# The last stage of a two-branch attention kernel: two layer-norm loops and an output loop merged into one loop over row tiles

## The chip, the cores and the metric

The kernel runs on one Trainium2 chip, the same program on eight cores, each with one batch element of 2048 rows by 1024 columns. The metric is the device time in microseconds (us) of the slowest core. The engines are TensorE (PE), VectorE (DVE), ScalarE (ACT), GpSimd (POOL) and SyncE (SP); here SP issues nearly all transfers. The profile is one execution on the slowest of the cores (core 5).

## The reference, cut to what matters

```python
xn = _layernorm(x, axis=-1)
s = _L0_attn_ref(xn, ...)          # 16 causal heads, then Wo, then a layer norm (eps 1e-5)
g = _silu(_L0_ffn_ref(xn, ...))    # six attention nodes of 8 heads, then a layer norm (eps 1e-6)
x = x + s * g
```

The last stage of the kernel computes, for each row, the layer norm of `y` (what the causal attention and its output product leave), the layer norm of `n5` (what the sixth node leaves), Silu of the second, their product, and the sum with the row of x.

## The kernel before, in words

Six nodes (projections, attention, output product) run first, then the causal attention ("L0"), then the product with Wo. Everything is kept feature-major, 128 features on the partitions and 2048 rows along them. Node 5 is stored to the DRAM tensor `n5_sp` and `y` to `y_sp`, both bf16 and feature-major. The trace calls `n5_sp` by the name `n_sp`.

The last stage starts when `y` is stored and has four parts, one behind the other.

1. `build_gam` (L1020 to L1038) spreads the norm's two parameter rows over the 128 partitions: for each row a 4 KB load into `lrow` (which is `fio[2]`), two matmuls with a row of ones into `ps[3]`, and two DVE copies into `gamT`. Each load waits for the copies of the row before it.
2. `ln_apply_loop` (L1040 to L1096) runs over the 16 row tiles of `y`. For each, SP issues a transposing load of 128 rows into `attb[0]` or `attb[1]` (L1043), DVE takes the sum (L1048) and the sum of squares (L1051, whose full result goes to PSUM as scratch), makes mean and variance in five operations on one column, ACT takes Ln and Exp of that column (L1073, L1076) for the reciprocal root, and DVE finishes with one small product (L1079) and three passes over the tile (L1082, L1086, L1090), the last into `slot[Dv]`. The load of tile tc waits for the last pass of tile tc-2.
3. `build_gam` and `ln_apply_loop` again, for `n5`, into the same `gamT` and into `slot[B]`; the first parameter load waits for all tiles of part 2.
4. All 16 Silu on ACT (L1105), and the output loop: load of 128 rows of x into `fio[0]` or `fio[1]` (L1112), product of the two norms into `fio[2]` (L1115), sum with x in place (L1118), store of `fio[2]` (L1122). The product of the next tile waits until the store has landed, because there is one `fio[2]`. The load of x for tile tc waits for the sum of tile tc-2, but it is issued on SP behind the store of tile tc-1, which waits for the sum of tile tc-1.

`P.op` (L46) appends an instruction to the list of its engine together with the waits it needs, and `finalize` (L72, the line that the waits carry in the trace is L73) writes each list out as it stands: a wait is an instruction of its own ahead of the operation. So every engine, SP and its transfers among them, works strictly in the order in which the Python code calls `P.op`. `trq` and `pln`, the names under which transfers are issued, are both `"sync"`.

`wstage` is a pair of fp32 staging tiles of 128 by 1024 for weights; by the last stage no weight is left to load.

Of the kernel before, what the change touches and what calls it, by code (L numbers as in the profile page):

```python
# [8 lines left out]
BF16 = mybir.dt.bfloat16  # L9
AF = mybir.ActivationFunctionType  # L10
ALU = mybir.AluOpType
AX = mybir.AxisListType

D = 1024
KC = 8
# [79 lines left out]
def build_nc(T=2048, debug=False):  # L95
    TC = T // 128
# [27 lines left out]
    n5_sp = nc.dram_tensor("n5_sp", [D, T], BF16, kind="Internal")  # L124
    y_sp = nc.dram_tensor("y_sp", [D, T], BF16, kind="Internal")
    dbg = {}
    if debug:
        for c in (0, 1):
# [11 lines left out]
    P = Prog()  # L140
# [5 lines left out]
    wstage = [e(nc.sbuf_tensor(f"wstage{i}", [128, 1024], F32)) for i in range(2)]  # L146
    qbuf = e(nc.sbuf_tensor("qbuf", [128, T], BF16))
    kbuf = e(nc.sbuf_tensor("kbuf", [128, T], BF16))
    attb = [e(nc.sbuf_tensor(f"attb{i}", [128, max(PW, 1024)], BF16))
            for i in range(4)]  # L150
# [17 lines left out]
    stat = e(nc.sbuf_tensor("stat", [128, 16], F32))  # L168
    gamT = e(nc.sbuf_tensor("gamT", [128, 2 * 1024], BF16))
# [4 lines left out]
    ps = [e(nc.psum_tensor(f"ps{i}", [128, 1024], F32)) for i in range(4)]  # L174
    ps_last = {0: None, 1: None, 2: None, 3: None}
# [4 lines left out]
    def slot_written(i, ch, tok):  # L180
        slot_w[i][ch] = tok if isinstance(tok, list) else [tok]
        slot_r[i] = []
# [11 lines left out]
    def tchunk(s, tc, d0=0, dw=1024):  # L194
        return slot[s][:, tc * 1024 + d0: tc * 1024 + d0 + dw]

    dge, pln, trq = "gpsimd", "sync", "sync"

    def pser():
# [4 lines left out]
        out=ewrow[0:1, 0:18],  # L204
        in_=W["few"].ap().rearrange("a b -> (a b)")[None, :]),
        waits=pser(), inc="P", inc_n=16)
    t_aw = P.op(trq, lambda g: g.dma_start(
        out=ewrow[0:1, 18:24], in_=W["fact"].ap()[None, :]),
        waits=pser(), inc="P", inc_n=16)
# [6 lines left out]
        waits=[t_io1], inc="tDVE")  # L216
    t_t128 = P.op("vector", lambda v: v.tensor_scalar(
        t128[:, :], fio[0][:, 0:128], 0.0, None, ALU.is_ge),
        waits=[t_io1], inc="tDVE")
# [6 lines left out]
        out=vec_stage[:, 0:128],  # L226
        in_=W["fbe"].ap().rearrange("a (c p) -> (a c) p", p=128)[0:128, :]),
        waits=pser(), inc="P", inc_n=16)
# [49 lines left out]
    for i in range(TC):  # L278
        b = i % 2
# [738 lines left out]
                               spill_sem="SPy")  # L1018
    wbuf_free[wo_b].append(t_y)

    def build_gam(i0, i1, ready):
        toks = []
        for j, i in enumerate((i0, i1)):
            tr = P.op(trq, lambda g, i=i: g.dma_start(
                out=lrow[0:1, 0:1024], in_=W[vps[4 + i]].ap()[None, :]),
                waits=pser() + list(ready) + toks, inc="P", inc_n=16)
            for h2 in range(2):
                tm = P.op("tensor", lambda t, j=j, h2=h2: t.matmul(
                    ps[3][:, h2 * 512:(h2 + 1) * 512], ones_f32r[0:1, :],
                    lrow[0:1, h2 * 512:(h2 + 1) * 512], start=True, stop=True),  # L1030
                    waits=[tr, ps_last[3], t_on2], inc="tPE")
                te = P.op("vector", lambda v, j=j, h2=h2: v.tensor_copy(
                    gamT[:, j * 1024 + h2 * 512: j * 1024 + (h2 + 1) * 512],
                    ps[3][:, h2 * 512:(h2 + 1) * 512]), waits=[tm], inc="tDVE")
                ps_last[3] = te
                toks.append(te)
        return toks

    def ln_apply_loop(dst_slot, src_sp, src_ready, eps, gam_toks):
        toks = []  # L1040
        for tc in range(TC):
            b = tc % 2
            tk = P.op(trq, lambda g, tc=tc, b=b, a=src_sp: g.dma_start(  # L1043
                out=attb[b][:, 0:1024], in_=a.ap()[:, tc * 128:(tc + 1) * 128],
                transpose=True),
                waits=list(src_ready) + attb_free[b], inc=f"T{b}", inc_n=16)
            q0 = 8 + b * 4
            t1 = P.op("vector", lambda v, b=b, q0=q0: v.reduce_sum(  # L1048
                stat[:, q0:q0 + 1], attb[b][:, 0:1024], axis=AX.X),
                waits=[tk] + list(gam_toks), inc="tDVE")  # L1050
            t4 = P.op("vector", lambda v, b=b, q0=q0: v.scalar_tensor_tensor(  # L1051
                ps[b][:, 0:1024], attb[b][:, 0:1024], 1.0,
                attb[b][:, 0:1024], ALU.mult, ALU.mult,
                accum_out=stat[:, q0 + 1:q0 + 2]),
                waits=[tk, ps_last[b]], inc="tDVE")
            ps_last[b] = t4
            tm = P.op("vector", lambda v, q0=q0: v.tensor_scalar(
                stat[:, q0:q0 + 1], stat[:, q0:q0 + 1], 1.0 / D, None,
                ALU.mult), waits=[t1], inc="tDVE")
            tq = P.op("vector", lambda v, q0=q0: v.tensor_tensor(  # L1060
                stat[:, q0 + 2:q0 + 3], stat[:, q0:q0 + 1],
                stat[:, q0:q0 + 1], ALU.mult), waits=[tm], inc="tDVE")
            tv = P.op("vector", lambda v, q0=q0: v.tensor_scalar(
                stat[:, q0 + 1:q0 + 2], stat[:, q0 + 1:q0 + 2], 1.0 / D,
                None, ALU.mult), waits=[t4], inc="tDVE")
            tv = P.op("vector", lambda v, q0=q0: v.tensor_tensor(
                stat[:, q0 + 1:q0 + 2], stat[:, q0 + 1:q0 + 2],
                stat[:, q0 + 2:q0 + 3], ALU.subtract),
                waits=[tv, tq], inc="tDVE")
            tv = P.op("vector", lambda v, q0=q0, eps=eps: v.tensor_scalar(  # L1070
                stat[:, q0 + 1:q0 + 2], stat[:, q0 + 1:q0 + 2], 1.0, eps,
                ALU.mult, ALU.add), waits=[tv], inc="tDVE")
            t6 = P.op("scalar", lambda s, q0=q0: s.activation(  # L1073
                stat[:, q0 + 2:q0 + 3], stat[:, q0 + 1:q0 + 2], AF.Ln),
                waits=[tv], inc="tACT")
            t7 = P.op("scalar", lambda s, q0=q0: s.activation(  # L1076
                stat[:, q0 + 1:q0 + 2], stat[:, q0 + 2:q0 + 3], AF.Exp,
                scale=-0.5), waits=[t6], inc="tACT")
            t7 = P.op("vector", lambda v, q0=q0: v.tensor_tensor(  # L1079
                stat[:, q0 + 3:q0 + 4], stat[:, q0:q0 + 1],  # L1080
                stat[:, q0 + 1:q0 + 2], ALU.mult), waits=[t7], inc="tDVE")
            t8 = P.op("vector", lambda v, b=b, q0=q0: v.tensor_scalar(  # L1082
                attb[b][:, 0:1024], attb[b][:, 0:1024],
                stat[:, q0 + 1:q0 + 2], stat[:, q0 + 3:q0 + 4],
                ALU.mult, ALU.subtract), waits=[t7], inc="tDVE")
            t9 = P.op("vector", lambda v, b=b: v.tensor_tensor(  # L1086
                attb[b][:, 0:1024], attb[b][:, 0:1024], gamT[:, 0:1024],
                ALU.mult), waits=[t8], inc="tDVE")
            t10 = P.op("vector", lambda v, b=b, ds=dst_slot, tc=tc:
                       v.tensor_tensor(  # L1090
                tchunk(ds, tc), attb[b][:, 0:1024], gamT[:, 1024:2048],
                ALU.add), waits=[t9], inc="tDVE")
            attb_free[b] = [t10]
            slot_written(dst_slot, tc % max(KC, TC), t10)
            toks.append(t10)
        return toks  # L1096

    fio_free[2] = ps_last[2]
    gam_s = build_gam(0, 1, y_spills)
    s_toks = ln_apply_loop(Dv, y_sp, y_spills, 1e-5, gam_s)  # L1100
    gam_g = build_gam(2, 3, s_toks)
    g_toks = ln_apply_loop(B, n5_sp, n5_spills, 1e-6, gam_g)
    gs_toks = []
    for tc in range(TC):
        gs_toks.append(P.op("scalar", lambda s, tc=tc: s.activation(  # L1105
            tchunk(B, tc), tchunk(B, tc), AF.Silu), waits=[g_toks[tc]],
            inc="tACT"))

    out_toks = []
    for tc in range(TC):  # L1110
        b = tc % 2
        tx = P.op(pln, lambda g, tc=tc, b=b: g.dma_start(  # L1112
            out=fio[b][:, :], in_=x_in.ap()[tc * 128:(tc + 1) * 128, :]),
            waits=[fio_free[b]], inc=f"X{b}", inc_n=16)
        t1 = P.op("vector", lambda v, tc=tc: v.tensor_tensor(  # L1115
            fio[2][:, :], tchunk(Dv, tc), tchunk(B, tc), ALU.mult),
            waits=[s_toks[tc], gs_toks[tc], fio_free[2]], inc="tDVE")
        t2 = P.op("vector", lambda v, b=b: v.tensor_tensor(  # L1118
            fio[2][:, :], fio[2][:, :], fio[b][:, :], ALU.add),
            waits=[tx, t1], inc="tDVE")  # L1120
        fio_free[b] = t2
        td = P.op(pln, lambda g, tc=tc: g.dma_start(  # L1122
            out=out_t.ap()[tc * 128:(tc + 1) * 128, :], in_=fio[2][:, :]),
            waits=[t2], inc="OUT", inc_n=16)
        fio_free[2] = td
        out_toks.append(td)
# [41 lines left out]
```

How the kernel before makes its waits and increments, by code:

```python
                def emit(eng):  # L70
                    for it in items:
                        if it[0] == "w":
                            eng.wait_ge(sems[it[1]], it[2])
                        else:
                            ins = it[1](eng)
                            if it[2] is not None:
                                ins.then_inc(sems[it[2]], it[3])
```

## Time and profile before

| | |
|---|---|
| runs of the kernel before | 7833.9 and 8154.16 us, median 7994.03 |
| the profiled execution | 7833.9 us |
| its span on the slowest core (5) | 7831.2 us |
| spans of the eight cores | 7773.6 to 7831.2 us |
| mean granted TensorE clock of the cores | 0.842 to 0.846 |
| the last stage on core 5, first parameter load to end of the span | 7500.8 to 7831.2, 330.4 us |
| busy over the span | PE 75%, PEld 24%, DVE 28%, ACT 35%, POOL 5% |

A row of the timeline gives the start in us, the duration in us, the engine, the line of the kernel, the operation, what it writes and reads, and in brackets how long the engine stood idle before it and what ended that. SPq is SP issuing a transfer: its duration is that of the issuing, not of the transfer.

### The profile page before, as it was taken

To read this page: it belongs to the slowest core of one execution; us is meant where nothing else is said; L and a number is where in the kernel's file an instruction comes from. 1 tells how busy PE (TensorE), PEld (TensorE's weight loads), DVE (VectorE), ACT (ScalarE), POOL (GpSimd) and SP (SyncE) were. 2 spreads that over 40 slices of the span, in tenths; PEclk is the share of its full clock that TensorE was granted. 3 is DMA by queue.
4 is the path that set the end of the run, shared out by engine and by line. 5 is a ranking of instruction groups with operands and counts; after the bars stand their busy time and mean duration, and the time that the engine had idled before them with its cause. 6 is when DMAs were issued, how large, how long until landed. Compare 5 with 4: busy or idle time off the path is not lost.

```text
span 7831.2 us, 62343 instructions; the slowest of 8 cores (7773.6 to 7831.2 us)
## 1 busy us (share of the span) xinstructions
PE 5850.8 (75%) x21827; PEld 1918.4 (24%) x21827; DVE 2198.8 (28%) x3068; ACT 2735.9 (35%) x2612; POOL 364.7 (5%) x354
## 2 busy tenths in 40 slices
PE   0677787777987779877789777897777878778830
PEld 0222233222332223322234222342222311111110
DVE  3133321333213332133321333213332122222155
ACT  0155432544225443155431454214552123333301
POOL 0100011000010000100011000110001100000000
PEclk9989998888998989988999888998888955555665
DMA  2300032000420004200033000230003100000013
GB/s 74 104 1 0 3 105 65 0 1 27 113 76 1 1 14 114 88 0 1 1 85 109 0 1 1 81 112 1 1 1 90 56 0 0 0 0 0 0 46 105
DMA packets 204568, 289.37 MB, mean 37 GB/s; under 512 B 141576, under 2 KB 141800, under 8 KB 204268
## 3 DMA queue, kind: packets, MB, share of 16 engines
q1 hardware_dynamic: 204236, 285.39, 12.4%
q8 instruction: 186, 3.05, 0.2%
q14 instruction: 114, 0.93, 0.0%
q0 software_dynamic: 32, 0.00, 0.0%
HBM read 218.24 MB, written 33.55 MB: 32 GB/s over the span
## 4 chain that ended last, share of the span: by engine, by line
PE 67%; DVE 18%; issue 6%; ACT 4%; DMA 4%; SPq 1%; DVEq 1%; POOL 0%; ACTq 0%; POOLq 0%
PE ps L384 17%; PE ps L564 9%; PE ps L869 8%; DVE attb L615 6%; PE ps L625 6%; PE ps L634 5%; PE ps L447 5%; PE ps L610 5%; DVE stat L515 4%; PE ps L595 3%; PE ps L586 3%; PE ps L508 3%; DVE attb L499 2%; DMA fio<-x 2%; ACT attb L675 1%
## 5 line engine op out<-in xcount | busy, mean ns | idle before, releaser
L675 ACT ACTIVATE attb<-ps,negM,scal 128x1024 bf16<-128x1024 f32 x1536 | 1766.8, 1199 | 1931.8 <-DVE negM L531 1435.6
L384 PE MATMUL ps<-slot,wbuf 128*128 128x512 bf16 x6144 | 1367.7, 383 | 223.3 <-POOL wbuf L358 199.2
L564 PE MATMUL ps<-qbuf,kbuf 128*128 128x512 bf16 x3072 | 1023.6, 424 | 173.0 <-ACT attb L675 150.2
L615 DVE TENSOR_TENSOR attb<-attb 128x1024 bf16<-128x1024 bf16 x768 | 534.8, 696 | 1787.6 <-PE ps L610 1771.7
L384 PEld LDWEIGHTS ps<-slot,wbuf 128*128 128x128 bf16 x6144 | 604.5, 99 | 971.8 <-issue 263.3
L869 PE MATMUL ps<-slot,wbuf 128*128 128x512 bf16 x3072 | 693.1, 385 | 82.8 <-POOL wbuf L358 82.8
L625 PE MATMUL ps<-attb,ones_bf 128*1 128x512 bf16 x1536 | 477.0, 393 | 360.6 <-DVE attb L615 354.9
L508 PE MATMUL ps<-attb,ones_sq 128*128 128x512 bf16 (+1 forms) x512 | 238.5, 564 | 609.6 <-DVE attb L499 608.4
L358 POOL CAST wbuf<-wstage 128x1024 bf16<-128x1024 f32 x344 | 363.1, 1059 | 5760.6 <-DVE kbuf L880 3655.9
L675 ACT ACTIVATE attb<-ps,negM 128x1024 bf16<-128x1024 f32 (+7 forms) x384 | 328.2, 863 | 664.0 <-PE ps L564 662.2
L610 PE MATMUL ps<-attb,slot 128*128 128x512 bf16 x1536 | 497.1, 408 | 21.3 <-DVE slot L737 21.3
L634 PE MATMUL ps<-attb,slot 128*128 128x512 bf16 x1536 | 481.5, 396 | 0.0
L564 PEld LDWEIGHTS ps<-qbuf,kbuf 128*128 128x128 bf16 x3072 | 278.6, 104 | 789.9 <-issue 632.4
L447 PE MATMUL ps<-wbuf,slot 128*128 128x512 bf16 x1792 | 394.3, 382 | 42.6 <-POOL wbuf L358 41.5
L515 DVE TENSOR_REDUCE stat<-ps 128x1 f32<-128x1024 f32 x256 | 313.6, 1225 | 391.2 <-PE ps L508 391.2
L869 PEld LDWEIGHTS ps<-slot,wbuf 128*128 128x128 bf16 x3072 | 299.8, 99 | 465.5 <-issue 122.2
L407 ACT ACTIVATE slot<-ps,beT 128x1024 bf16<-128x1024 f32 x120 | 133.7, 1114 | 700.6 <-PE ps L384 700.6
L564 PE MATMUL ps<-slot 64*128 64x512 bf16 x768 | 361.6, 579 | 16.7 <-ACT attb L675 16.5
L415 DVE TENSOR_SCALAR slot<-ps,beT 128x1024 bf16<-128x1024 f32 x120 | 154.1, 1284 | 721.6 <-PE ps L384 721.6
L880 DVE CAST qbuf<-ps 128x1024 bf16<-128x1024 f32 x96 | 117.6, 1225 | 678.6 <-PE ps L869 678.6
L595 PE MATMUL ps<-attb,slot 128*64 128x512 bf16 (+3 forms) x656 | 294.1, 530 | 0.0
L586 PE MATMUL ps<-attb,ones_bf 128*1 128x512 bf16 (+3 forms) x656 | 283.2, 514 | 2.3 <-DVE attb L686 2.3
(101 smaller groups left out, 2531.4 us busy)
## 6 DMA issues: line engine op xcount, KB each, us to landing
wstage<-fWe SPq DMA_DIRECT2D x120, 512.0 KB, 4.3
wstage<-fWv SPq DMA_DIRECT2D x48, 512.0 KB, 4.2
wstage<-fWq SPq DMA_DIRECT2D x48, 512.0 KB, 4.2
wstage<-fWk SPq DMA_DIRECT2D x48, 512.0 KB, 4.1
wstage<-fWo SPq DMA_DIRECT2D x48, 512.0 KB, 4.2
slot<-n_sp SPq DMA_DIRECT2D x40, 512.0 KB, 9.0
fio<-x SPq DMA_DIRECT2D x32, 512.0 KB, 4.1
n_sp<-slot SPq DMA_DIRECT2D x32, 512.0 KB, 2.6
```

The lines of the kernel that those rows point to most:

```text
L384: t.matmul(ps[pb][:, sg * SEG:(sg + 1) * SEG], wtile(ws, kc, do * 128, 128), fchunk(ss, kc, th * TW + sg * SEG, SEG), start=(kc == 0), sto ...
L447: pb=pb, ws=wslot, ss=src_slot: t.matmul(ps[pb][:, half * 512:(half + 1) * 512], fchunk(ss, kc, tc * 128, 128), wtile(ws, kc, half * 512, ...
L515: t_mx = P.op("vector", lambda v, dst=dst: v.reduce_max(stat[:, dst:dst + 1], ps[3][:, 0:NH], axis=AX.X), waits=[t_nm], inc="tDVE")
L564: t_s = P.op("tensor", lambda t, kc=kc, sg=sg, pb=pb: t.matmul(ps[pb][:, sg * PSEG:(sg + 1) * PSEG], kf_tile_fn(kc), q_rhs_fn(sg * PSEG, P ...
L586: l_first=l_first, l_last=l_last: t.matmul(ps[3][0:1, o:o + w], ones_bf[:, 0:1], attb[ab][:, o:o + w], start=l_first, stop=l_last),
L595: av_stop=av_stop: t.matmul(ps[2][obase:obase + dh, o:o + w], v_tile_fn(kc), attb[ab][:, o:o + w], start=av_first, stop=av_stop, tile_posi ...
L610: first=(j0 == 0): t.matmul(ps[2][obase:obase + dh, o:o + w], v_tile_fn(kc0), attb[a0][:, o:o + w], start=first, stop=False, tile_position ...
L615: t_pr = P.op("vector", lambda v, a0=a0, a1=a1: v.tensor_tensor(attb[a0][:, 0:PW], attb[a0][:, 0:PW], attb[a1][:, 0:PW], ALU.add), waits=[ ...
L625: t.matmul(ps[3][0:1, o:o + w], ones_bf[:, 0:1], attb[a0][:, o:o + w], start=first, stop=last),
L634: last=(j1 == n_kc - 1): t.matmul(ps[2][obase:obase + dh, o:o + w], v_tile_fn(kc1), attb[a1][:, o:o + w], start=False, stop=last, tile_pos ...
L675: off=off: s.activation(attb[ab][:, off:PW], ps[pb][:, off:PW], AF.Exp, bias=negM[:, nc_:nc_ + 1], scale=scale_col),
L869: src_sl=src_sl: t.matmul(ps[pb][:, sg * SEG:(sg + 1) * SEG], wtile(wsl, kc, h * 128, 128), fchunk(src_sl, kc, th * TW2 + sg * SEG, SEG), ...
```

## The change

The three loops of the last stage become one. For each row tile the new loop norms the tile of `y` (`ln_tile` with `attb[0]`/`attb[1]`, `ps[0]`/`ps[1]`, statistics in columns 0 to 7), norms the tile of `n5` (with `attb[2]`/`attb[3]`, `ps[2]`/`ps[3]`, columns 8 to 15), takes Silu of it, loads x, multiplies, adds and stores. Both parameter pairs are spread ahead of the loop; the second pair goes into `gamT2`, which is `wstage[0]` read as bf16. The operations on a tile are the same as before, in the same order within a tile; the order over the tiles, and with it each engine's list and SP's list of transfers, is new. The wait for the parameters moves from the sum (L1048) to the transposing load.

```diff
+    gamT2 = wstage[0].ap().bitcast(BF16)
-    def ln_apply_loop(dst_slot, src_sp, src_ready, eps, gam_toks):
-        toks = []
-        for tc in range(TC):
-            b = tc % 2
-            tk = P.op(trq, lambda g, tc=tc, b=b, a=src_sp: g.dma_start(
-                out=attb[b][:, 0:1024], in_=a.ap()[:, tc * 128:(tc + 1) * 128],
-                transpose=True),
-                waits=list(src_ready) + attb_free[b], inc=f"T{b}", inc_n=16)
...
+    def ln_tile(dst_slot, src_sp, src_ready, eps, g0, g1, tc, ab, psb, q0,
+                gtoks):
+        b = tc % 2
+        tk = P.op(trq, lambda g, tc=tc, ab=ab, a=src_sp: g.dma_start(
+            out=attb[ab][:, 0:1024], in_=a.ap()[:, tc * 128:(tc + 1) * 128],
+            transpose=True),
+            waits=list(src_ready) + attb_free[ab] + list(gtoks),
+            inc=f"T{ab}", inc_n=16)
...
-    gam_s = build_gam(0, 1, y_spills)
-    s_toks = ln_apply_loop(Dv, y_sp, y_spills, 1e-5, gam_s)
-    gam_g = build_gam(2, 3, s_toks)
-    g_toks = ln_apply_loop(B, n5_sp, n5_spills, 1e-6, gam_g)
-    gs_toks = []
-    for tc in range(TC):
-        gs_toks.append(P.op("scalar", lambda s, tc=tc: s.activation(
-            tchunk(B, tc), tchunk(B, tc), AF.Silu), waits=[g_toks[tc]],
-            inc="tACT"))
+    gam_s = build_gam(0, 1, y_spills, lambda j, h2: gamT[
+        :, j * 1024 + h2 * 512: j * 1024 + (h2 + 1) * 512])
+    gam_g = build_gam(2, 3, list(n5_spills) + gam_s, lambda j, h2: gamT2[
+        :, j * 1024 + h2 * 512: j * 1024 + (h2 + 1) * 512],
+        wgate=[wstage_free[0]])
+    fio_free[2] = gam_g[-1]
 
     out_toks = []
     for tc in range(TC):
         b = tc % 2
+        s_tok = ln_tile(Dv, y_sp, y_spills, 1e-5, gamT[:, 0:1024],
+                        gamT[:, 1024:2048], tc, b, b, b * 4, gam_s)
+        g_tok = ln_tile(B, n5_sp, n5_spills, 1e-6, gamT2[:, 0:1024],
+                        gamT2[:, 1024:2048], tc, 2 + b, 2 + b, 8 + b * 4,
+                        gam_g)
+        gs_tok = P.op("scalar", lambda s, tc=tc: s.activation(
+            tchunk(B, tc), tchunk(B, tc), AF.Silu), waits=[g_tok],
+            inc="tACT")
         tx = P.op(pln, lambda g, tc=tc, b=b: g.dma_start(
             out=fio[b][:, :], in_=x_in.ap()[tc * 128:(tc + 1) * 128, :]),
             waits=[fio_free[b]], inc=f"X{b}", inc_n=16)
         t1 = P.op("vector", lambda v, tc=tc: v.tensor_tensor(
             fio[2][:, :], tchunk(Dv, tc), tchunk(B, tc), ALU.mult),
-            waits=[s_toks[tc], gs_toks[tc], fio_free[2]], inc="tDVE")
+            waits=[s_tok, gs_tok, fio_free[2]], inc="tDVE")
```

The sum and the store that follow are as before.

## Rows read from the trace of the kernel before

**Rows 1.** The page: span, and the chain that ended last, by engine.
```profile
span 7831.2 us, 62343 instructions; the slowest of 8 cores (7773.6 to 7831.2 us)
...
PE 67%; DVE 18%; issue 6%; ACT 4%; DMA 4%; SPq 1%; DVEq 1%; POOL 0%; ACTq 0%; POOLq 0%
```

**Rows 2.** Busy time by stretch: PE, PEld, DVE, ACT, POOL; clock, DMA share, GB/s.
```profile
7516.10:7617.20 101.10, 0.00 (x0) 0.00 (x0) 79.53 (x192) 6.49 (x32) 0.00 (x0) 0.50 0.18 37
...
7632.60:7734.60 102.00, 0.00 (x0) 0.00 (x0) 79.43 (x192) 8.87 (x35) 0.00 (x0) 0.50 0.19 41
7734.60:7831.20 96.60, 0.00 (x0) 0.00 (x0) 39.28 (x33) 14.15 (x15) 0.00 (x0) 0.50 0.50 168
```

**Rows 3.** Timeline of the first norm loop: tiles 0 and 1 of `y`.
```profile
7516.12 1.22 DVE L1048 TENSOR_REDUCE stat<-attb 128x1 f32<-128x1024 bf16 x1
...
7519.26 0.15 DVE L1070 TENSOR_SCALAR stat<-stat 128x1 f32<-128x1 f32 x1
7519.51 0.20 ACT L1073 ACTIVATE stat<-stat 128x1 f32<-128x1 f32 x1 [28.60 <-DVE stat L1070]
...
7521.90 0.69 DVE L1090 TENSOR_TENSOR slot<-attb,gamT 128x1024 bf16<-128x1024 bf16 x1
7522.50 1.21 DVE L1048 TENSOR_REDUCE stat<-attb 128x1 f32<-128x1024 bf16 x1
```

**Rows 4.** Timeline of the output loop: tiles 0 and 1, and the last sum.
```profile
7734.66 1.23 DVE L1115 TENSOR_TENSOR fio<-slot 128x1024 f32<-128x1024 bf16 x1
7735.99 1.23 DVE L1118 TENSOR_TENSOR fio<-fio 128x1024 f32<-128x1024 f32 x1
7737.29 0.37 SPq L1122 DMA_DIRECT2D out<-fio  x1
7737.71 0.42 SPq L1112 DMA_DIRECT2D fio<-x  x1
...
7742.52 1.23 DVE L1118 TENSOR_TENSOR fio<-fio 128x1024 f32<-128x1024 f32 x1 [1.03 <-DMA fio<-x]
...
7826.92 1.23 DVE L1118 TENSOR_TENSOR fio<-fio 128x1024 f32<-128x1024 f32 x1 [0.38 <-DMA fio<-x]
```

**Rows 5.** Waits of the last stage: who waited for what, us, times, longest.
```profile
DVE fio L1115 <- DMA out<-fio: 42.6, 14, 3.1
DVE stat L1079 <- ACT stat L1076: 22.6, 32, 1.0
DVE fio L1118 <- DMA fio<-x: 8.5, 15, 1.0
```

**Rows 6.** Timeline around the second parameter spread.
```profile
7617.27 0.25 SPq L1024 DMA_DIRECT2D fio<-fln_g  x1
...
7632.65 1.22 DVE L1048 TENSOR_REDUCE stat<-attb 128x1 f32<-128x1024 bf16 x1
```

**Rows 7.** The transposing load's own view: issue ns min/median/max, time to landing.
```profile
L1043 SPq DMA_TRANSPOSE attb<-y_sp x16: 1145/1146/1207, 7508.8 to 7604.6; - x16
...
DMA to landing us min/median/max: 2.9/3.2/4.4
```

**Rows 8.** The page's transfers: the node reloads, KB each, us to landing.
```profile
slot<-n_sp SPq DMA_DIRECT2D x40, 512.0 KB, 9.0
```

**Rows 9.** Timeline around the only two table loads of the kernel.
```profile
36.60 0.15 DVE L308 TENSOR_SCALAR stat<-stat 128x1 f32<-128x1 f32 x1
36.84 1.28 ACT L311 ACT_TABLE_LOAD   x1 [36.84 <-DVE stat L308]
...
38.73 0.16 DVE L317 TENSOR_TENSOR stat<-stat 128x1 f32<-128x1 f32 x1 [1.98 <-ACT stat L314]
...
7731.99 0.20 ACT L1076 ACTIVATE stat<-stat 128x1 f32<-128x1 f32 x1
7732.21 1.28 ACT L1105 ACT_TABLE_LOAD   x1
...
7733.51 15.25 ACT L1105 ACTIVATE slot<-slot 128x1024 bf16<-128x1024 bf16 x16
```

More of the change, by code:

```diff
@@ L1019, in build_nc, with build_gam @@
     wbuf_free[wo_b].append(t_y)
-    def build_gam(i0, i1, ready):
+    gamT2 = wstage[0].ap().bitcast(BF16)
+    def build_gam(i0, i1, ready, dst_fn, wgate=()):
         toks = []
@@ L1027, in build_gam @@
             for h2 in range(2):
-                tm = P.op("tensor", lambda t, j=j, h2=h2: t.matmul(
+                tm = P.op("tensor", lambda t, h2=h2: t.matmul(
                     ps[3][:, h2 * 512:(h2 + 1) * 512], ones_f32r[0:1, :],
@@ L1032, in build_gam @@
                 te = P.op("vector", lambda v, j=j, h2=h2: v.tensor_copy(
-                    gamT[:, j * 1024 + h2 * 512: j * 1024 + (h2 + 1) * 512],
-                    ps[3][:, h2 * 512:(h2 + 1) * 512]), waits=[tm], inc="tDVE")
+                    dst_fn(j, h2), ps[3][:, h2 * 512:(h2 + 1) * 512]),
+                    waits=[tm] + list(wgate), inc="tDVE")
                 ps_last[3] = te
@@ L1037, in build_gam @@
         return toks
-    def ln_apply_loop(dst_slot, src_sp, src_ready, eps, gam_toks):
-        toks = []
-        for tc in range(TC):
-            b = tc % 2
-            tk = P.op(trq, lambda g, tc=tc, b=b, a=src_sp: g.dma_start(
-                out=attb[b][:, 0:1024], in_=a.ap()[:, tc * 128:(tc + 1) * 128],
-                transpose=True),
-                waits=list(src_ready) + attb_free[b], inc=f"T{b}", inc_n=16)
[L1047 to L1096, printed above, removed]
@@ L1098, in build_nc @@
-    fio_free[2] = ps_last[2]
-    gam_s = build_gam(0, 1, y_spills)
-    s_toks = ln_apply_loop(Dv, y_sp, y_spills, 1e-5, gam_s)
-    gam_g = build_gam(2, 3, s_toks)
-    g_toks = ln_apply_loop(B, n5_sp, n5_spills, 1e-6, gam_g)
-    gs_toks = []
-    for tc in range(TC):
-        gs_toks.append(P.op("scalar", lambda s, tc=tc: s.activation(
-            tchunk(B, tc), tchunk(B, tc), AF.Silu), waits=[g_toks[tc]],
-            inc="tACT"))
+    def ln_tile(dst_slot, src_sp, src_ready, eps, g0, g1, tc, ab, psb, q0,
[6 more added lines that the diff above has]
+            inc=f"T{ab}", inc_n=16)
+        t1 = P.op("vector", lambda v, ab=ab, q0=q0: v.reduce_sum(
+            stat[:, q0:q0 + 1], attb[ab][:, 0:1024], axis=AX.X),
+            waits=[tk], inc="tDVE")
+        t4 = P.op("vector", lambda v, ab=ab, q0=q0, psb=psb:
+                  v.scalar_tensor_tensor(
+            ps[psb][:, 0:1024], attb[ab][:, 0:1024], 1.0,
+            attb[ab][:, 0:1024], ALU.mult, ALU.mult,
+            accum_out=stat[:, q0 + 1:q0 + 2]),
+            waits=[tk, ps_last[psb]], inc="tDVE")
+        ps_last[psb] = t4
+        tm = P.op("vector", lambda v, q0=q0: v.tensor_scalar(
+            stat[:, q0:q0 + 1], stat[:, q0:q0 + 1], 1.0 / D, None,
+            ALU.mult), waits=[t1], inc="tDVE")
+        tq = P.op("vector", lambda v, q0=q0: v.tensor_tensor(
+            stat[:, q0 + 2:q0 + 3], stat[:, q0:q0 + 1],
+            stat[:, q0:q0 + 1], ALU.mult), waits=[tm], inc="tDVE")
+        tv = P.op("vector", lambda v, q0=q0: v.tensor_scalar(
+            stat[:, q0 + 1:q0 + 2], stat[:, q0 + 1:q0 + 2], 1.0 / D,
+            None, ALU.mult), waits=[t4], inc="tDVE")
+        tv = P.op("vector", lambda v, q0=q0: v.tensor_tensor(
+            stat[:, q0 + 1:q0 + 2], stat[:, q0 + 1:q0 + 2],
+            stat[:, q0 + 2:q0 + 3], ALU.subtract),
+            waits=[tv, tq], inc="tDVE")
+        tv = P.op("vector", lambda v, q0=q0, eps=eps: v.tensor_scalar(
+            stat[:, q0 + 1:q0 + 2], stat[:, q0 + 1:q0 + 2], 1.0, eps,
+            ALU.mult, ALU.add), waits=[tv], inc="tDVE")
+        t6 = P.op("scalar", lambda s, q0=q0: s.activation(
+            stat[:, q0 + 2:q0 + 3], stat[:, q0 + 1:q0 + 2], AF.Ln),
+            waits=[tv], inc="tACT")
+        t7 = P.op("scalar", lambda s, q0=q0: s.activation(
+            stat[:, q0 + 1:q0 + 2], stat[:, q0 + 2:q0 + 3], AF.Exp,
+            scale=-0.5), waits=[t6], inc="tACT")
+        t7 = P.op("vector", lambda v, q0=q0: v.tensor_tensor(
+            stat[:, q0 + 3:q0 + 4], stat[:, q0:q0 + 1],
+            stat[:, q0 + 1:q0 + 2], ALU.mult), waits=[t7], inc="tDVE")
+        t8 = P.op("vector", lambda v, ab=ab, q0=q0: v.tensor_scalar(
+            attb[ab][:, 0:1024], attb[ab][:, 0:1024],
+            stat[:, q0 + 1:q0 + 2], stat[:, q0 + 3:q0 + 4],
+            ALU.mult, ALU.subtract), waits=[t7], inc="tDVE")
+        t9 = P.op("vector", lambda v, ab=ab, g0=g0: v.tensor_tensor(
+            attb[ab][:, 0:1024], attb[ab][:, 0:1024], g0,
+            ALU.mult), waits=[t8], inc="tDVE")
+        t10 = P.op("vector", lambda v, ab=ab, g1=g1, ds=dst_slot, tc=tc:
+                   v.tensor_tensor(
+            tchunk(ds, tc), attb[ab][:, 0:1024], g1,
+            ALU.add), waits=[t9], inc="tDVE")
+        attb_free[ab] = [t10]
+        slot_written(dst_slot, tc % max(KC, TC), t10)
+        return t10
```

## The prediction

> **What bounds the kernel now.** I read the page first. Over the whole span the chain that ended last is mostly PE, with DVE second [rows 1]; but the change touches nothing ahead of the last stage, so the share that counts is that stage's own, 330.4 of 7831.2 us. The windows cut by its parts come next: 101.1 us for the norm of `y`, 102.0 for the norm of `n5`, 96.6 for the output loop [rows 2], and two parameter spreads of 15.4 us each (7617.27 to 7632.65, [rows 6]; the first runs from 7500.8 to 7516.1 in the same way). PE does nothing in the three loops. Then the timeline, loop by loop.
>
> In the norm loops DVE is busy 79.5 of 101.1 us [rows 2], one tile takes 101.1/16 = 6.32 us, and the one wait of any size is for Ln and Exp (22.6 us over 32 tiles, 0.71 each, [rows 5]). The loads cost nothing: two pairs of buffers let them run a tile ahead. So these loops are bound by DVE's own list.
>
> The output loop is different. DVE is busy 39.3 of 96.6 us there. From the first sum at 7735.99 to the last at 7826.92 there are 15 pitches of 6.06 us [rows 4], of which the product and the sum take 2.5; 42.6 us go to waiting for the store of the one `fio[2]` and 8.5 to waiting for x [rows 5]. SP issues the store, then the next load of x, which lands after the store does: issue at 7737.71, sum at 7742.52. This loop is bound by one turn of DMA per tile. That is what a merged loop can hide, and the sum has to show what it exposes in exchange.
>
> **Cost per part.** *Parameters.* The second spread is not removed, it moves ahead of the loop. It still waits for the first one's copies, nothing runs beside it, and it still takes 15.4 us. The first load of `y` is queued behind its second row's load on SP and lands while the copies still run. The first sum then starts at 7516.12 + 15.4 = 7531.5. Against before: nothing gained, nothing lost.
>
> *Norm of a tile.* Same instructions. From the start of the first sum to the end of the last pass is 7516.12 to 7521.90 + 0.69, that is 6.47 us [rows 3]; where another tile follows, 6.32.
>
> *Product, sum, x and store.* 1.33 to the sum's start, 1.23 for the sum, 2.56 together [rows 4]. The store has a whole tile of DVE work to land in, and x is loaded at the head of the tile: both waits of [rows 5] go. That removes (42.6 + 8.5) us plus the tile-0 wait for Silu.
>
> *The transposing load.* Here the cover goes. SP's list is now: load `y`(tc), load `n5`(tc), x(tc), store(tc), load `y`(tc+1). The store waits for the sum of tile tc, the last thing DVE does in a tile, and everything behind it on SP waits too, although `attb` is free long before. DVE's next instruction is the sum over `y`(tc+1), so DVE and ACT stand still for a whole turn. Its length: 0.07 from the end of the sum to the store (7737.22 to 7737.29), 0.42 until the next transfer can be issued (7737.71) [rows 4], the landing, and 0.1 to DVE. A landing took 2.9 to 4.4 us, median 3.2 [rows 7], but mostly with the queue idle; here a 512 KB store is just ahead and a second transpose just behind. Below, 2.9 us; above, the 4.4 plus 1.5, since the output loop moves two such transfers per 6.06 us at a DMA share of 0.50, so one keeps the engines for 0.25 x 6.06 = 1.5 us [rows 2, 4]. I take 3.8, nearer the median, because issuing a transpose alone takes 1.15 us [rows 7], in which most of the store drains. Together 4.4 us per tile, 15 times (tile 0 is covered by the parameters). The load of `n5` is issued 1.15 us later and needed 7 us later: hidden.
>
> *Table loads.* Before, ACT did all Ln and Exp, then one table load, then 16 Silu. The kernel has two table loads, of 1.28 us, Ln and Exp sharing one table [rows 9]. Now Silu of tile tc stands between Exp of tile tc and Ln of tile tc+1: one load before each Silu, 16, and one before each Ln but the first, 15. Are they hidden while ACT idles? The first load says no: ACT stood idle for 36.84 us, with nothing to do, and began the load only when DVE's column came, because the load sits behind the wait; DVE then waited 1.98 us for the result in place of the usual 0.7 [rows 5, 9]. So each of the 31 is on the path at 1.28 us. Below, nothing, if they ran ahead of the wait. Above, I take a second load's time per switch, 1.28 more. I choose 1.28, as both loads in the trace are followed at once by their ACTIVATE (7732.21 + 1.28, next at 7733.51).
>
> On this the Trainium skill speaks against the change. "ScalarE: Activation LUTs", section "Rules for kernel authors", says to group functions by table set, and "What ACT_TABLE_LOAD costs" gives 1283 ns for the load plus about 1380 ns of drain, 2.66 us per switch. The trace agrees on the 1.28 and shows no drain: the load at 7732.21 starts 0.02 us after Exp ends. By the page's figure the estimate would be 31 x 1.38 = 43 us more than mine.
>
> *Silu.* Before, 15 of 16 ran under the output loop's stalls (15.25 us for 16, [rows 9]). Now the product waits for its own: 0.1 from DVE to ACT (as L1070 to L1073, [rows 3]), 1.30 for load and start, about 1.0 for one ACTIVATE (15.25/16 = 0.95 in a row, a little more for one alone), 0.1 back: 2.5 us.
>
> **The sum.** A tile takes 4.39 (SP, store, load) + 6.32 + 1.28 (norm of `y` with a table load) + 6.47 (norm of `n5`) + 2.50 (Silu) + 2.56 = 23.52 us. Before, the same work took (7828.15 - 7516.12 - 15.5)/16 = 18.5 us per tile over the three loops. Tile 0 has neither the load wait nor the first table load: 17.85. The last sum ends at 7531.5 + 17.85 + 15 x 23.52 = 7902.2; before it ended at 7828.15. That is 74 us more. Hiding the transfers of the output loop gives back 6.06 - 2.56 = 3.5 us per tile; the exposed transposing load costs 4.4, the two table loads 2.6, the uncovered Silu 1.2, and the last 0.3 are ends that no longer overlap.
>
> The profiled execution took 7833.9 us, so I expect 7833.9 + 74 = 7908 us, 0.94% more. The shown median, 7994.03, lies halfway between two runs that are 320 us apart; the profiled one is the lower. Ahead of the last stage nothing changes, so the same shift holds for either: 8068 on the median.
>
> **Rivals.**
>
> *A. As summed*, small loss, 7908; with the transpose at 2.9 or at 5.9 and everything else the same, 15 x 0.9 = 14 less, 7894, or 15 x 2.1 = 32 more, 7940.
>
> *B. Table loads hidden.* If they ran ahead of the wait during ACT's idle time, 31 x 1.28 = 40 us less: 7868. For it: ACT is idle in most of each tile. Against: the load at 36.84 [rows 9].
>
> *C. Each switch costs twice the load.* 40 us more: 7948. For it: the trace has no case of a load between Silu and Ln, and only two loads. Against: no gap beside either. The skill's rule above is this case, with its 1.38.
>
> *D. Not slower: the transposes run ahead.* If SP issued the load of tile tc+1 before the store of tile tc, the 4.4 us go: the tile is 19.13, the end at 7531.5 + 17.85 + 15 x 19.13 = 7836.3, 8 us later than before, 7842, which no one can tell from before. It decides at a per-tile pitch of 18.5. Against it: SP's list as `finalize` writes it, and the same order in the output loop, where x waits behind the store each time [rows 4]. If the change were to win, this is where, and even then the table loads eat it.
>
> *E. Slower by over 2%.* That needs 157 us, 83 beyond my sum, 5.5 per tile: the transpose would have to land in 9.3 us. Transfers in this kernel do land as late as 9.0 us in the median, where many 512 KB loads are queued [rows 8]. With 9.0 it is 7833.9 + 74 + 15 x 5.2 = 7986. Against it: there is but one store ahead here, and the DMA share falls from 0.50 to less than half of that.
>
> **How the numbers follow.** A 0.66, B 0.10, C 0.12, D 0.04, E 0.04; 0.04 for what I have not seen. The likeliest is A, 7908, and its own range is 7890 to 7945. For 8 in 10 the range takes in B and C, 7860 below and 7965 above. The shown times of before are a median over runs so far apart that the time after may be one too; the like shift of that median gives 8068, so I set the upper end at 8085. About 2% is what a measurement of this kernel can tell from no change: A to D lie within it, E lies at its edge, and the spread of the runs adds a little. Faster 0.02, within 0.90, slower 0.08.
>
> **What would show each step.** In the profile after: 32 table loads in all, each beginning when DVE's column or tile arrives; DVE waiting about 2 us for Exp in the norm of `y` and 0.7 in that of `n5`; the product waiting about 2.5 us for Silu and never for the store; the sum never waiting for x; SP issuing store, transpose, transpose, x in one bunch per tile, and the first DVE sum of a tile about 4.4 us behind the last sum; a pitch of about 23.6 us; the stage from the first parameter load to the end about 405 us in place of 330. I would be wrong if the pitch came out at or under 18.5, if the table loads started while ACT idled, or if the landing of a transpose were doubled by the store.

## The result and the profile after

The changed kernel is slower by 1%: the ratio of its time to that of the kernel before is 1.0098, with a 95% interval of 1.0078 to 1.0118. Five of its executions took 7904 to 7910 us, and the profiled one of before 7833.9 us. The medians over all executions, 8026.66 us (14) against 8154.16 (12), point the other way only because they hold executions in which the cores of one die ran at a lower granted clock (the profiled one of the changed kernel is such a one, 0.824 to 0.831 on cores 0 to 3); the ratio leaves those out.

The profile after is read on core 5: span 7904.3 us, clock 0.841. To compare last stages, one measure serves for all kernels: from the issue of the last store of `y` to the end of the span. It is 333.9 us before (mean of the eight cores, 329.9 to 335.9) and 410.3 after (407.9 to 412.2). TensorE does little in this stage, and its length does not follow the clock: 409.0 to 412.2 us on cores 0 to 3, 407.9 to 411.3 on cores 4 to 7 (0.836 to 0.841). The last stage holds 76.4 us of difference; 0.98% of 7834 is 77. So the stage accounts for the whole loss as closely as it is known, and nothing ahead of the stage was changed.

Busy time by stretch on core 5 of the changed kernel: the parameter spreads, then the merged loop (columns as in [rows 2]).

```profile
7496.88:7527.22 30.34, 16.33 (x16) 3.98 (x16) 5.45 (x8) 0.00 (x0) 0.00 (x0) 0.50 0.05 10
7527.22:7904.30 377.08, 0.00 (x0) 0.00 (x0) 199.51 (x417) 69.65 (x111) 0.00 (x0) 0.50 0.24 66
```

DVE works about as long as before (199.5 us against 79.5 + 79.4 + 39.3 in [rows 2]), in 377 us instead of 300. ACT is busy for 69.7 us, where it was busy for 29.5. The DMA share is 0.24 in the mean, where the output loop alone had 0.50.

The waits of the changed kernel, on core 5, from the last store of `y` to the end:

```profile
ACT L1075 <- DVE stat L1072: 159.5, 15, 11.0
ACT stat L1075 <- DVE stat L1072: 139.1, 17, 45.1
DVE stat L1049 <- DMA attb<-y_sp: 68.1, 15, 4.9
DVE fio L1121 <- ACT slot L1115: 41.5, 16, 2.6
DVE stat L1081 <- ACT stat L1078: 41.4, 32, 2.0
```

Against [rows 5]: the waits for the store and for x are gone, all 51 us. In their place DVE waits 68.1 us for the transposes of `y`, 41.5 us for Silu, and 41.4 instead of 22.6 for Exp. One turn from tile to tile, in the timeline of core 5:

```profile
7657.59 0.69 DVE L1092 TENSOR_TENSOR slot<-attb,wstage 128x1024 bf16<-128x1024 bf16 x1
7658.36 1.28 ACT L1115 ACT_TABLE_LOAD   x1 [2.59 <-DVE slot L1092]
7659.66 1.06 ACT L1115 ACTIVATE slot<-slot 128x1024 bf16<-128x1024 bf16 x1
7660.89 1.23 DVE L1121 TENSOR_TENSOR fio<-slot 128x1024 f32<-128x1024 bf16 x1 [2.60 <-ACT slot L1115]
7662.22 1.23 DVE L1124 TENSOR_TENSOR fio<-fio 128x1024 f32<-128x1024 f32 x1
7663.51 0.34 SPq L1128 DMA_DIRECT2D out<-fio  x1
7663.90 1.50 SPq L1044 DMA_TRANSPOSE attb<-y_sp  x1
7665.44 1.27 SPq L1044 DMA_TRANSPOSE attb<-n_sp  x1
7666.75 0.56 SPq L1118 DMA_DIRECT2D fio<-x  x1
7668.37 1.22 DVE L1049 TENSOR_REDUCE stat<-attb 128x1 f32<-128x1024 bf16 x1 [4.93 <-DMA attb<-y_sp]
...
7671.75 1.28 ACT L1075 ACT_TABLE_LOAD   x1 [11.03 <-DVE stat L1072]
...
7673.64 0.16 DVE L1081 TENSOR_TENSOR stat<-stat 128x1 f32<-128x1 f32 x1 [1.97 <-ACT stat L1078]
```

Read it for who stands still. After the last pass over the tile, DVE has nothing until Silu is done, and Silu starts with a table load. After the sum at 7662.22 DVE has nothing again: SP wakes, issues the store, and only then the transpose that DVE needs next. The bracket of the second table load is the telling one: ACT had been idle for 11.03 us and still began the load only when DVE's column arrived. Each of these gaps is in series with the next, because each engine has one list and the tile's last operation stands ahead of the next tile's first in all of them.

### The profile page after: what moved, and what is told of

It is laid out like the page before. It is cut to its first block, busy times and chain, and to the rows that moved or that the text cites. A ratio compares the mean times of both kernels' runs of the same rounds, so it can differ in the third digit from the quotient of the medians.

```text
span 8000.8 us, 62361 instructions; the slowest of 8 cores (7861.0 to 8000.8 us)
## 1 busy us (share of the span) xinstructions
PE 5947.4 (74%) x21827; PEld 1942.7 (24%) x21827; DVE 2200.4 (28%) x3068; ACT 2778.9 (35%) x2642; POOL 364.9 (5%) x354
## 4 chain that ended last, share of the span: by engine, by line
PE 67%; DVE 18%; issue 6%; ACT 4%; DMA 3%; SPq 1%; DVEq 1%; POOL 0%; ACTq 0%; POOLq 0%
PE ps L384 17%; PE ps L564 9%; PE ps L869 8%; DVE attb L615 6%; PE ps L625 6%; PE ps L447 5%; PE ps L634 5%; PE ps L610 5%; DVE stat L515 4%; PE ps L595 3%; PE ps L586 3%; PE ps L508 3%; DVE attb L499 2%; ACT attb L675 1%; DMA wstage<-fWk 1%
## 5 line engine op out<-in xcount | busy, mean ns | idle before, releaser
L384 PE MATMUL ps<-slot,wbuf 128*128 128x512 bf16 x6144 | 1413.5, 393 | 220.3 <-POOL wbuf L358 196.3
L869 PE MATMUL ps<-slot,wbuf 128*128 128x512 bf16 x3072 | 709.9, 391 | 79.3 <-POOL wbuf L358 79.3
L447 PE MATMUL ps<-wbuf,slot 128*128 128x512 bf16 x1792 | 412.6, 394 | 44.2 <-POOL wbuf L358 43.2
```

The costliest lines, as they stand in the source:

```text
L384: t.matmul(ps[pb][:, sg * SEG:(sg + 1) * SEG], wtile(ws, kc, do * 128, 128), fchunk(ss, kc, th * TW + sg * SEG, SEG), start=(kc == 0), sto ...
L447: pb=pb, ws=wslot, ss=src_slot: t.matmul(ps[pb][:, half * 512:(half + 1) * 512], fchunk(ss, kc, tc * 128, 128), wtile(ws, kc, half * 512, ...
L869: src_sl=src_sl: t.matmul(ps[pb][:, sg * SEG:(sg + 1) * SEG], wtile(wsl, kc, h * 128, 128), fchunk(src_sl, kc, th * TW2 + sg * SEG, SEG), ...
```

## The experiments

The theory is the prediction's: three costs in series on DVE's path, namely the turn of the transpose behind the store (SP's order), 31 table loads that sit behind their waits, and Silu without cover. Against it stand three others: that the transposes are late from traffic, that table loads cost twice their own time or nothing, and that the merged loop as such, or the new place of the parameters, costs time. The stage in each heading is the mean over the eight cores of one execution, in the measure above; where a ratio to the kernel before is given, it is that of whole executions.

**The parameters alone (stage 334.3 us).** The kernel before, with both spreads ahead of its three loops.

```diff
-    gam_s = build_gam(0, 1, y_spills)
-    s_toks = ln_apply_loop(Dv, y_sp, y_spills, 1e-5, gam_s)
-    gam_g = build_gam(2, 3, s_toks)
-    g_toks = ln_apply_loop(B, n5_sp, n5_spills, 1e-6, gam_g)
+    gam_s = build_gam(0, 1, y_spills, gamT)
+    gam_g = build_gam(2, 3, list(n5_spills) + gam_s, gamT2,
+                      [wstage_free[0]])
...
+    s_toks = ln_apply_loop(Dv, y_sp, y_spills, 1e-5, gam_s, gamT)
+    g_toks = ln_apply_loop(B, n5_sp, n5_spills, 1e-6, gam_g, gamT2)
```

> The kernel before with one part of the change alone: both parameter spreads ahead of the loops, the second into the weight staging tile; the three loops stay. Theory: the 15.4 us move and nothing else changes, the stage stays at 330 us within 1 us. Rival: the staging tile as a source of the norm's last two passes is slower on DVE, or the early spread overlaps with something; then the passes over it take other than 0.69 us or the stage moves by more than 3 us.

Measured 334.3 us against 333.9. The move of the spread, and the staging tile as the home of the second pair, cost and bring nothing that shows. What is left for the 76.4 us is the order within the merged loop.

**Transposes ahead of the store (stage 340.9 us).**

```diff
     tx = P.op(pln, ... out=fio[b][:, :], in_=x_in ...)     # tile tc
+    if tc + 1 < TC:
+        load_pair(tc + 1)      # both transposing loads of the next tile
     t1 = ...; t2 = ...
     td = P.op(pln, ... out=out_t ..., in_=fio[2][:, :])    # store of tile tc
```

> The changed kernel with one edit: the two transposing loads of tile tc+1 are issued on SP before the store of tile tc instead of behind it. Theory (serial turn): in the changed kernel DVE waits 68.1 us over 15 tiles for the transpose of y because it is queued behind the store; issued earlier it lands under the norm, so that wait goes to 0, the last stage shrinks from 407.4 to about 339 us, the pitch from 23.75 to 19.2 us, and the kernel comes out about 9 us over the kernel before, ratio 1.001. Rival (contention): the transposes are late because of the traffic beside them, wherever they are issued; then part of the wait comes back as a wait for x or for the transpose of n5, and the stage stays above 370 us, ratio 1.005 or more.

Measured 340.9 us, 69.5 less than the changed kernel, where 68.1 us of waiting were to go; ratio to the kernel before 1.0005 (0.9989 to 1.002). The timeline around one tile's end, on core 5:

```profile
7639.43 1.22 DVE L1133 TENSOR_TENSOR fio<-fio 128x1024 f32<-128x1024 f32 x1
7640.57 1.21 DVE L1049 TENSOR_REDUCE stat<-attb 128x1 f32<-128x1024 bf16 x1
7640.73 0.34 SPq L1137 DMA_DIRECT2D out<-fio  x1
...
7641.59 1.72 SPq L1042 DMA_TRANSPOSE attb<-y_sp  x1
7643.35 2.11 SPq L1042 DMA_TRANSPOSE attb<-n_sp  x1
7643.94 1.28 ACT L1075 ACT_TABLE_LOAD   x1 [6.01 <-DVE stat L1072]
```

The sum over the next tile starts at 7640.57, without a bracket: no wait at all, 0.16 us before the store is even issued. The transposes now take longer to issue (1.72 and 2.11 us, against 1.15 in [rows 7]), with a store and a load of x on the queue ahead of them, and they land later too: for `y` 5.2 us after the start of their issue in the median, against 3.9 in the changed kernel and 3.2 before. It doesn't matter, since they have a whole tile to land in. So traffic does slow them; where they stand in the list is what costs. This is also the prediction's rival D, carried out: the kernel comes out level with before, and the table loads, untouched here, eat the gain.

**Table loads (stages 371.0 and 371.1 us).** First, with one-element ACTIVATEs that draw each load forward:

```diff
+        e_s = P.op("scalar", lambda s: s.activation(
+            tiny[0:1, 13:14], ones_f32r[0:1, 0:1], AF.Silu), waits=[e_s], ...)
         gs_tok = P.op("scalar", ... AF.Silu), waits=[g_tok], inc="tACT")
+        if tc + 1 < TC:
+            e_l = P.op("scalar", lambda s: s.activation(
+                tiny[0:1, 14:15], ones_f32r[0:1, 0:1], AF.Ln), waits=[e_l], ...)
```

> The changed kernel with tiny ACTIVATEs added on ACT: a Silu of one element ahead of the wait for the normed tile, and an Ln of one element right behind the tile's Silu, so that both table loads can run while ACT has nothing to do. Full computation is kept. Theory (the load sits behind the wait): all 31 loads leave the path, DVE waits 0.7 us for Exp and 1.3 us for Silu per tile, the stage goes from 407.4 to about 367 us, ratio to the kernel before about 1.005. Rival (each switch costs 2.66 us, load and drain): 82 us off, stage 325. Rival (loads are hidden already or cannot overlap): stage stays at 407.

Second, with a function that brought no table load into the stage, so that Silu is left out:

```diff
-            tchunk(B, tc), tchunk(B, tc), AF.Silu), waits=[g_tok], inc="tACT")
+            tchunk(B, tc), tchunk(B, tc), AF.Copy), waits=[g_tok], inc="tACT")
```

> The changed kernel with Silu replaced by a Copy of the same size; the gate of the second branch is left out, so the output is another one. Copy needs no table of its own, so there are no table switches. Theory (1.28 us per switch): 31 x 1.28 = 40 us off, stage 367 us, the product waits 1.3 us for ACT in place of 2.6. Rival (load and drain, 2.66 us per switch): 82 us off, stage 325. Rival (loads hidden): stage stays at 407.

Both come to the same: 39.4 and 39.3 us less than the changed kernel, 1.27 us per switch over 31 switches. The first has the ratio 1.0064 (1.0018 to 1.0109). Its timeline on core 5 shows the loads moved into idle time:

```profile
7645.62 0.20 ACT L1078 ACTIVATE stat<-stat 128x1 f32<-128x1 f32 x1
7645.85 1.28 ACT L1116 ACT_TABLE_LOAD   x1
...
7647.14 0.20 ACT L1116 ACTIVATE tiny<-ones_f32r 1x1 f32<-1x1 f32 x1
7648.43 1.06 ACT L1119 ACTIVATE slot<-slot 128x1024 bf16<-128x1024 bf16 x1 [1.09 <-DVE slot L1092]
7649.51 1.28 ACT L1123 ACT_TABLE_LOAD   x1
7649.66 1.22 DVE L1129 TENSOR_TENSOR fio<-slot 128x1024 f32<-128x1024 bf16 x1 [1.32 <-ACT slot L1119]
```

The load follows Exp by 0.03 us and is over before DVE delivers the tile; the product waits 1.32 us where it waited 2.60. Nothing costs more than the load's own 1.28 us: the 82 us that a switch of 2.66 us would have given back were not there, even in the second kernel, which does not switch in the stage at all. The Trainium skill ("ScalarE: Activation LUTs", section "What ACT_TABLE_LOAD costs") gives 1283 ns for the load and about 1380 ns of drain on top. The load is what was measured here; a drain added to it does not show.

**Both (stage 301.6 us).** The two edits together.

> The changed kernel with both edits: transposes of the next tile issued ahead of the store, and one-element Silu and Ln that draw the table loads into ACT's idle time. Theory: the two costs are in series on DVE's path and add up, 68 + 40 = 108 us off, stage about 299 us, pitch 16.6 us, about 31 us under the kernel before, ratio 0.996. Rival (they overlap, one covers the other): the stage stays at or above 330 us.

Measured 301.6 us, 108.8 less than the changed kernel; one by one they had given 69.5 and 39.4, in sum 108.9. These two costs are in series, neither hides the other. On core 5 the wait for Exp is back at 22.6 us for 32 and that for Silu at 21.1 for 16. The fastest execution took 7800.42 us; no interval for its ratio was obtained.

**The product one tile late (stage 301.2 us).** Transposes ahead, here by two tiles, and the product, sum and store of tile tc-1 (`finish`) placed behind the norms of tile tc; the table loads are left where they are.

```diff
+    load_pair(0)
+    load_pair(1)
+    for tc in range(TC):
...
+        pend[tc] = (s_tok, gs_tok, tx)
+        if tc + 2 < TC:
+            load_pair(tc + 2)
+        if tc >= 1:
+            finish(tc - 1)
+    finish(TC - 1)
```

> The changed kernel with the transposes issued ahead and the product, the sum and the store of a tile moved one tile later, so that Silu and its table load run under the norms of the next tile. Theory: transposes and Silu are off the path; the table load before Ln stays on it only as far as ACT is not done by then. DVE's own work is 2 x 6.32 + 2.56 = 15.2 us per tile, plus 1.28 for the load before Ln: pitch 16.5 us, stage about 297 us. Rival (in-order ACT now delays Ln behind Silu by more than that): pitch above 17.8.

Measured 301.2 us (300.6 to 302.0), 4 over what was expected. Of the one execution of this kernel, at a granted clock of 0.803 to 0.815, only the stage is used. The pitch was right (two sums over `y` tiles stand 16.34 us apart, at 7811.88 and 7828.22 on core 5). What I left out is the end of the list, where the last two tiles finish one behind the other and the one `fio[2]` makes the last product wait 2.8 us for a store. On core 5 the last tile takes 25.1 us from its first sum to the end, 8.6 over the expected pitch of 16.5, and the first tile, which has no product in it, 3.8 less. Silu and the load before it vanish from DVE's waits altogether; the load before Ln stays, as the Exp row shows (41.5 us, as in the changed kernel). This sizes the third cost: with the transposes ahead alone the product waited 41.5 us for Silu and its table load, and the stage was 39.7 us longer than here.

**Two output tiles in the kernel before (stage 290.6 us).** Here the loops are not merged. The output loop gets a second output tile and a third tile for x, and x is loaded two tiles ahead of the store.

```diff
+    obuf = [fio[2], wstage[0]]
+    xbuf = [fio[0], fio[1], wstage[1]]
...
+        if tc + 2 < TC:
+            load_x(tc + 2)
         t1 = P.op("vector", ... obuf[o] ..., waits=[s_toks[tc], gs_toks[tc], ofree[o]])
```

> The kernel before with its three loops kept and only the output loop's buffers changed: two output tiles (the free weight staging tile is the second), three tiles for x, and x loaded two tiles ahead of the store. Theory (the output loop waited on one buffer and on SP's order): the waits for the store (42.6 us) and for x (8.5 us) mostly go; 1 MB per tile still needs about 3.0 us of all DMA engines against 2.5 us of DVE, so the pitch falls from 6.06 to about 3.1 us, the loop from 96.6 to about 52 us, the stage from 330 to about 286, ratio 0.994. Rival (eight cores at once saturate the memory at the 168 GB/s each that the loop moved): the pitch stays above 5 us, and only merging could hide the transfers.

Measured 290.6 us, 43.3 less than before, ratio 0.9953 (0.9919 to 0.9987). The waits of that loop on core 5:

```profile
DVE wstage L1128 <- DMA out<-wstage: 6.3, 7, 2.0
DVE fio L1128 <- DMA out<-fio: 2.9, 5, 0.8
```

9.2 us instead of 51 [rows 5]. Busy time from the end of its first sum to the start of its last, in the columns of [rows 2]:

```profile
7721.97:7768.65 46.68, 0.00 (x0) 0.00 (x0) 35.37 (x31) 11.54 (x13) 0.00 (x0) 0.50 0.88 310
```

The loop moved 168 GB/s per core before [rows 2] and moves 310 here: it was not short of bandwidth, but of buffers and of a better place in SP's list for x. The run does not part the second output tile from the third tile and the earlier loads of x. At a DMA share of 0.88 what still waits is probably the transfers themselves.

**A version that beats both (stage 255.4 us).** All of it in the merged loop: transposes ahead, product one tile late, table loads drawn forward, and the four parameter rows spread by transfers and GpSimd casts while the product with Wo still runs.

```diff
+    gload = [P.op(trq, lambda g, i=i: g.dma_start(
+        out=gbuf[i][:, :],
+        in_=W[vps[4 + i]].ap()[None, :].broadcast_to([128, 1024])), ...)
+        for i in range(4)]
...
+    for i in range(4):
+        gt_ = gamT if i < 2 else gT2
+        gcast.append(P.op("gpsimd", lambda g, i=i, gt_=gt_: g.tensor_copy(
+            gt_[:, (i % 2) * 1024:(i % 2 + 1) * 1024], gbuf[i][:, :]), ...))
```

> A version meant to beat both: transposes ahead, product one tile late, one-element Silu and Ln for the table loads, and the four parameter rows spread by transfers that repeat a row over the partitions and cast by GpSimd while the product with Wo still runs, in place of the 30.8 us of loads, matmuls and copies ahead of the loop. Theory: pitch 15.2 us, 16 tiles in 243 us, about 8 us at the two ends, stage about 251 us from the end of the last store of y, about 79 us under the kernel before, ratio 0.990. Rival (the spreading transfers or the casts disturb the product with Wo, or the table loads cannot be drawn forward): the stage is 270 us or more, or the product before it is longer by more than 10 us.

Measured 255.4 us (254.8 to 256.9), 78.5 under before; ratio to the kernel before 0.9879 (0.9812 to 0.9945). The casts are the whole of what GpSimd does for it, and they lie early in the product with Wo, which runs from 7382.0 to the last store of `y` at 7440.4 on core 5 and takes as long as before (58.3 us in the mean of the cores against 58.4):

```profile
7387.20 1.04 POOL L1027 CAST gamT<-fio 128x1024 bf16<-128x1024 f32 x1 [1184.74 <-DMA fio<-agamma]
...
7390.91 1.04 POOL L1027 CAST wstage<-wstage 128x1024 bf16<-128x1024 f32 x1 [0.19 <-DMA wstage<-fln_b]
```

**The same without the parameters (stage 282.2 us), and without the merging (stage 264.7 us).** The first takes the parameters out again, to size them. The second asks whether merging is worth anything: three loops, two output tiles, parameters by transfer.

> The merged version with the parameters still spread by loads, matmuls and copies ahead of the loop; all else as in the version that is meant to beat both. Theory: the spreads are 30.5 us in series with the rest, and the first transpose lands under them; the stage is 255.4 + 30.5 - 5.9 (the wait for the first transpose) = 280 us, pitch 15.2 us. Rival (the casts and transfers under the product with Wo cost as much as they save): 262 us or less.

Measured 282.2 us, where 280 was expected. The parameters are worth 26.8 us net. On core 5 the first sum begins 33.2 us behind the last store of `y` with the spreads ahead of it, and 5.8 us behind it without them, where DVE waits for the first transpose.

> Does merging the loops pay at all? The kernel before with its three loops, two output tiles and early loads of x, and the parameter rows spread by transfers and GpSimd casts during the product with Wo; only Silu in one batch at the end of the norms, so one table load. Theory (merging hid nothing that a second output tile doesn't): the stage is the 290.6 us of the three loops with two output tiles less the 30.5 us of the two parameter spreads, plus the landing of the first transpose, about 3 us: 260 to 264 us, within 8 us of the merged version's 255.4, ratio to the kernel before about 0.991. Rival (the merged loop hides transfers that the separate output loop can't): 275 us or more.

Measured 264.7 us (262.4 to 267.1), just above the 260 to 264 expected, ratio 0.9902 (0.9873 to 0.9931). Merging, done well, is worth 9.3 us of the stage beyond it, by one execution of each, on different chips; in the whole time that is 0.1%, and no ratio between the two was measured. What it hides is likely the waits for the store, 14.4 us on core 5 (in the rows below), of which the merged version has 2.8; no run takes that apart.

```profile
DVE fio L1126 <- DMA out<-fio: 7.7, 7, 1.5
DVE wstage L1126 <- DMA out<-wstage: 6.7, 7, 1.4
```

## Why the prediction was right in its mechanism and wrong in what it said of the result

*The terms.* All of them were found in the trace, on core 5:

| term | predicted | measured |
|---|---|---|
| first sum after the second spread begins | 15.4 us | 15.0 us (7512.20 to 7527.22) |
| turn of the transpose, per tile | 4.39 us | 4.54 us (68.1/15) |
| landing of the transpose | 3.8 us | median 3.9 us (the 15 of `y` behind a store) |
| wait for Exp in the norm of `y` | 0.7 + 1.28 us | 1.97 us |
| wait for Silu, per tile | 2.5 us | 2.60 us |
| pitch of the loop | 23.52 us | 23.75 us ((7900.05 - 7543.84)/15) |
| last stage, more than before | 74 us | 76.4 us |
| whole kernel | +0.94% | +0.98% (0.78 to 1.18) |

The turn, 0.15 us longer than predicted, makes 2.3 us of the 2.4 that the stage was over. The prediction's two worries on size, a transpose landing at 5.9 us or a switch at twice its load, did not come. That the landing met the 3.8 is in part luck: the reason given for it, that most of the store drains while the transpose is issued, was tested by no run, and with a load of x ahead as well the same transpose took 5.2 us. Every sign that it named for the profile after is there: 32 table loads in all, 31 of them in the stage, each begun when DVE delivers; no wait for the store, none for x; one bunch of four transfers per tile.

*The step that failed* is the last of the sum, from the 74 us to the time: "The profiled execution took 7833.9 us, so I expect 7833.9 + 74 = 7908 us". The headline stands on the lower of the two runs of before. It is 1.1% below the shown median of 7994.03, and so reads as a gain, though the sum says that the kernel loses. The runs showed a loss: the ratio is 1.0098, which excludes no change. On the shown median the same sum gives 8068, which the text names only in passing. As a time of an execution the 7908 was close (six of the 14 took 7904 to 7926 us); as a forecast against the number shown it points the wrong way. With two runs 320 us apart the honest number is the ratio, and the headline has to be given on the base that it will be read against.

The step behind it, from the time to the statement, failed too. The text says that "about 2% is what a measurement of this kernel can tell from no change" and puts 0.90 on "within". As it is worded that came true, 0.98% lies within 2%; its reason did not hold. The interval of the ratio is 0.2% to either side, so a loss of 1% stands five of these clear of none. The two runs could not show how fine the comparison would be, but the sum itself had one sign on any base, and the forecast should have said "slower, by 1%".

*The rivals.* D, the transposes running ahead, did not occur by itself; it was priced at 8 us over before, and carried out it gave 340.9 - 333.9 = 7.0 us. B, hidden table loads, did not occur either; priced at 40 us, it gave 39.4 when carried out. C and E did not occur. What the prediction did not see is how much could be had: it priced the output loop's stalls at 3.5 us per tile as a thing to be hidden by merging, when a second output tile, a third tile for x and earlier loads of x took 43.3 us of it away without merging.

*Open.* How much of the transpose's 3.9 us is due to the store ahead of it was not separated from the share of the second transpose behind it; only that neither matters once both have a tile's time. Not tried was to issue the stores from another engine than SP, which would also take the transposes out from behind them.

## What to carry to other kernels

When loops are merged tile by tile, write out each engine's list for two tiles in a row, transfers included: whatever the next tile needs first must not stand behind what this tile does last, so issue loads a tile ahead and put the tail of a tile behind the head of the next. Count how often an engine changes function tables in the merged order; each change cost 1.27 us on the path here, and a one-element ACTIVATE of the next function, ahead of the wait, took it off. Before merging to hide a stalled loop, try it with more buffers and earlier loads: that took 43 us off here, of 51 us of waits.

## What the runs showed of the hardware that I had not expected

A table load started only once the wait ahead of its ACTIVATE was met, in the changed kernel after up to 11.03 us of idle ACT. It did not wait for the tile as such: behind a one-element ACTIVATE it ran 0.03 us after Exp and under DVE's passes over the tile. Issuing a transposing load of `y` took SP 1.15 us with nothing just ahead on the queue, 1.50 behind a store, and 1.73 behind a store and a load of x (medians); the one of `n5` right behind it took 1.27 and 2.30 in the last two cases, up to 2.88.
